# Splitting a mixture-of-experts pass at the tenth weight half: a first pass under a scan, a pass over all tokens, and a rest

## The reference

```python
u  = x @ Wi.T + bi;  sp = x @ Ws.T + bs             # 128 states
def step(state, inp):                               # one after the other, 2048 times
    u_t, sp_t = inp
    state = jnp.tanh(state @ A.T + u_t @ B.T) + sp_t
    return (state, state @ C.T)
x = layernorm(x + ys @ Wo.T + bo)
# experts: D = 1024, H = 4096, E = 8, the two best by softmax of x @ gate_w.T
h = relu(einsum('nd,edh->neh', x, w1) + b1)
y = einsum('neh,eho->neo', h, w2) + b2
x = layernorm(x + einsum('ne,neo->no', dense_gate, y))
# layer 1: causal attention with 16 heads, then a gated feed-forward
```

## Time and profile before

| | us |
|---|---|
| two runs | 8627.08 and 8993.85, median 8810.46 |
| profiled execution | 8637.14 |
| its span, slowest core (1) | 8635.5 |
| spans of its cores | 8619.6 to 8635.5 |

### The profile page before, as it was taken

How to read it: one execution, slowest core, us unless ns; L and a number is a source line. 1 busy time by engine, 2 the same in 40 slices (tenths; PEclk the granted TensorE clock), 3 DMA queues, 4 the chain that set the end, 5 groups by cost and what they waited for, 6 DMA issues and landing times.

```text
span 8635.5 us, 83834 instructions; the slowest of 8 cores (8619.6 to 8635.5 us)
## 1 busy us (share of the span) xinstructions
PE 5770.1 (67%) x24427; PEld 2317.4 (27%) x24427; DVE 2788.6 (32%) x4299; ACT 1541.8 (18%) x3342; POOL 431.5 (5%) x676
## 2 busy tenths in 40 slices
PE   2256666676648989888889899834556455645545
PEld 1122222222223434333333344311112111211111
DVE  0021111111232222222222222244554555445555
ACT  2312222222200010100100101012112211221111
POOL 0001111111000000000000000000000000000000
PEclk6579899899859999999999999965556555555677
DMA  1035555555313222233232222210000000000012
GB/s 45 0 52 77 77 78 77 78 77 78 65 27 49 41 40 40 40 48 50 48 49 41 40 40 40 40 11 5 10 10 6 5 10 10 6 5 5 0 19 50
DMA packets 181047, 321.74 MB, mean 37 GB/s; under 512 B 67222, under 2 KB 67734, under 8 KB 178582
## 3 DMA queue, kind: packets, MB, share of 16 engines
q0 software_dynamic: 170240, 284.34, 21.9%
q1 hardware_dynamic: 10390, 32.04, 1.2%
HBM read 583.71 MB, written 8.39 MB: 69 GB/s over the span
## 4 chain that ended last, share of the span: by engine, by line
PE 43%; DMA 27%; DVE 15%; issue 8%; ACT 5%; DVEq 1%; ACTq 0%; POOLq 0%; SPq 0%; PEldq 0%
PE psA L1024 37%; DMA w1b<-w 12%; DMA w2c<-w 8%; DMA w1f<-w 6%; PE psB L1024 6%; DVE mcols L1024 4%; ACT tanh_bf L1024 2%; ACT PT L1024 2%; DVE xA L1024 2%; DVE Qpair L1024 1%; DVE qraw L1024 1%; DVE mtmp L1024 1%; DVE rowT L1024 1%; DVE mcol L1024 1%; ACT rowT L1024 1%
## 5 line engine op out<-in xcount | busy, mean ns | idle before, releaser
L1024 PE MATMUL psA<-xS,w1b 128*128 128x512 bf16 x7168 | 1716.6, 388 | 353.8 <-DMA w1b<-w 344.2
L1024 PE MATMUL psA<-hbuf,w2c 128*128 128x512 bf16 x8192 | 1785.1, 380 | 70.5 <-DVE hbuf L1024 70.5
L1024 DVE TENSOR_SCALAR hbuf<-psA,b1c 128x512 bf16<-128x512 f32 x512 | 384.5, 751 | 2590.1 <-PE psA L1024 2590.1
L1024 PEld LDWEIGHTS psA<-hbuf,w2c 128*128 128x128 bf16 x8192 | 791.7, 98 | 1040.2 <-issue 100.2
L1024 PEld LDWEIGHTS psA<-xS,w1b 128*128 128x128 bf16 x7168 | 682.7, 99 | 1123.3 <-issue 418.2
L1024 ACT ACTIVATE tanh_bf<-psB,c_n 128x1 bf16<-128x1 f32 x2047 | 538.8, 263 | 1428.6 <-PE psB L1024 1428.6
L1024 PE MATMUL psB<-tanh_bf,AT_s 128*128 128x1 bf16 x2047 | 336.4, 164 | 493.3 <-ACT tanh_bf L1024 452.7
L1024 ACT ACTIVATE hbuf<-psA,b1c 128x512 bf16<-128x512 f32 x512 | 351.8, 687 | 1279.7 <-PE psA L1024 1264.2
L1024 PE MATMUL psA<-xS,w1f 128*128 128x512 bf16 x1024 | 340.5, 392 | 257.4 <-DMA w1f<-w 248.0
L1024 ACT ACTIVATE PT<-psA 128x512 bf16<-128x512 f32 (+3 forms) x448 | 308.6, 689 | 1023.2 <-PE psA L1024 1011.4
L1024 PEld LDWEIGHTS psB<-tanh_bf,AT_s 128*128 128x128 bf16 x2047 | 201.5, 98 | 1049.8 <-issue 1037.8
(11 more groups left out here) (155 smaller groups left out, 3787.5 us busy)
## 6 DMA issues: line engine op xcount, KB each, us to landing
w2c<-w POOLq DMA_DIRECT2D x256, 512.0 KB, 5.3
w1b<-w POOLq DMA_DIRECT2D x192, 512.0 KB, 5.3
w1f<-w POOLq DMA_DIRECT2D x128, 256.0 KB, 4.2
xA<-xT SPq DMA_DIRECT2D x8, 1024.0 KB, 16.7
out<-ost SPq DMA_DIRECT2D x8, 1024.0 KB, 12.7
xA<-xT SPq DMA_DIRECT2D x8, 768.0 KB, 13.2
Qh<-Qpair SPq DMA_DIRECT2D x16, 256.0 KB, 3.4
Kh<-Qpair SPq DMA_DIRECT2D x16, 256.0 KB, 3.4
```

Source lines behind the costliest of these rows:

```text
L1024: ins = getattr(eng_obj, method)(*args, **kw)
```

## The change

The first pass over tile 0 stops after KA = 10 of the 16 halves. Then scan output, norm and gate of tiles 1 to 3 are done as before, and the rest comes in two calls: the last six halves for all four tiles, and the first ten halves for tiles 1 to 3. `moe` takes the tiles, the list of halves and `pp` as arguments. The 1536 scan steps are spread over 10 x 152 = 1520 hooks instead of 16 x 152 = 2432. A call that finds earlier matmuls makes its first w1 load wait for them. Every token still meets every half once; six of the 32 loads of a half are gone (26 are left).

```diff
     CH_NTS = ((0,), (1, 2, 3))
+    KA = 10
...
-    def moe(ch, hook=None):
-        nts = CH_NTS[ch]
-        pp = (ch == 0)
+    def moe(nts, halves, pp, hook=None):
         w1done = {}
         zw = (("zin", V("zin")),)
-        w1_load(HALVES[0][0], HALVES[0][1], w=zw)
+        if V("mm1") > 0:
+            zw = zw + (("mm1", V("mm1")),)
+        w1_load(halves[0][0], halves[0][1], w=zw)
         w1done[0] = V("w1l")
         mm2_slice = None
-        for hi, (e, half) in enumerate(HALVES):
+        for hi, (e, half) in enumerate(halves):
...
-            if pp and hi + 1 < len(HALVES):
-                e2, h2 = HALVES[hi + 1]
+            if pp and hi + 1 < len(halves):
+                e2, h2 = halves[hi + 1]
...
-            if not pp and hi + 1 < len(HALVES):
-                e2, h2 = HALVES[hi + 1]
+            if not pp and hi + 1 < len(halves):
+                e2, h2 = halves[hi + 1]
                 w1_load(e2, h2, w=(("mm1", V("mm1")),))
...
-            mark(f"moe_c{ch}")
-            nhooks = 16 * len(CH_NTS[0]) * (16 * 9 + 8)
-            per = [0]
-
-            def hook(per=per, ch=ch):
-                if ch == 0:
+            if ch == 0:
+                mark("moe_c0")
+                nhooks = KA * (16 * 9 + 8)
+                per = [0]
+
+                def hook(per=per):
                     per[0] += 1
                     tgt = TS + ((T - TS) * per[0]) // nhooks
                     scan_pump(tgt - scan_cursor[0])
-            moe(ch, hook=hook)
-            if ch == 0:
+                moe(CH_NTS[0], HALVES[:KA], pp=True, hook=hook)
                 scan_pump(T - scan_cursor[0])
+            else:
+                mark("moe_mix")
+                moe((0, 1, 2, 3), HALVES[KA:], pp=False)
+                mark("moe_c1")
+                moe(CH_NTS[1], HALVES[:KA], pp=False)
             barrier()
```

## The result

| | before | after |
|---|---|---|
| median of all runs, us | 8792.71 (29 runs) | 8740.86 (30 runs) |
| lowest, us | 8624.07 | 8545.44 |
| profiled execution, us | 8637.14 | 8575.5 |
| spans of its cores, us | 8619.6 to 8635.5 | 8535.9 to 8574.1 |

The ratio after to before is **0.9927, with a 95% interval of 0.9895 to 0.9959**: a small gain, 0.7%, well inside the 2% named in the prediction. Forecast was 8557 / 8637 = 0.9907, which lies in the interval. But 8741, the median, lies above the range given, 8490 to 8660. The two medians hold executions in which the cores of one die, or of both, were granted a lower clock, and which take up to 9137.97 and 9126.2 us; the ratio leaves them out. The two lowest times differ by 78.6 us.

A forecast was written before the change was run, and what follows sets the result against it. The load queue was taken to bound the first phase, the scan's chain after the change. Saving 422.0 us there and adding 341.9 in mixed halves gives -80.1 on the profiled 8637.14: 8557 us, range 8490 to 8660.

The forecast's parts named there:

- What bounds the kernel, and what comes next: First phase: bound passes from loads, 109.7 us a half, to the scan's chain, 130.9 us a half on PE.
- Loads hidden: First phase: loads cost nothing; tightest is w1f of half 1, with 6 us to spare.
- Clock: First phase: clock may fall in w1 stages, costing 2.4 us per half at the w2 stage start, 24 in all.
- a thinner stage costs nothing in itself: First-phase w1 stages: at the lower clock a step with one large matmul behind it still takes 0.67 us.
- Mixed halves: Six halves with four tiles: one more tile each at 56.98 us, 341.9 us added, nothing new exposed.
- Seams: Starts of the mixed phase and of the last ten halves: taken as nothing, bounded by 8 us.
- dense stretch: Rival, chance 0.05: mixed halves' longer dense PE work, 230 us against 173, is throttled; 342 us more, 8899 us.
- The rest of the kernel taken as untouched: Stages between the phases and all after them: unchanged, 0 us.
- The time itself and its range: Whole kernel: 8557 us for an execution like the profiled one, range 8490 to 8660, 0.5% for the spread of runs.
- the late loads: Rival, chance 0.05: in the first phase w1f arrives late on five halves, 155 us more, 8712 us.
- the low clock: Rival, chance 0.06: clock stays low through ten first-phase w2 stages, up to 27.8 us each, 278 in all, 8811 us.
- the first rival: Rival, chance 0.04: loads still set the first phase's pace, which would save 658 us there, 8321 us.

The follow-up runs named there:

- scan-first run: The changed kernel with all remaining 1536 scan steps made before the ten halves instead of between their matmuls; spans of 9158.8 to 9170.6 us.
- spread run: The changed kernel with a scan hook also after each of the 128 w2 matmuls; 8338.23 us at best, timed again 8365.16 us median, ratio 0.9656.
- thirteen halves: The changed kernel with thirteen first-phase halves instead of ten, three mixed, gate row fetched at the first half of every call; ratio 0.9873 to the kernel before.
- warm: The changed kernel with one unused 128x512 matmul into an idle PSUM bank after each w1 matmul of the first phase; ratio 0.9859 to the kernel before.
- eight-half split: The changed kernel with eight halves in the first phase instead of ten and eight in the mixed one; ratio 0.9959 to the kernel before.
- ka13warm: The split at thirteen halves with one unused 128x512 matmul after every fourth w1 matmul of the first phase; ratio 0.9903 to the kernel before.

## Why the prediction was right in its parts and wrong in its time

| term, us (core 5 against core 1 before) | predicted | measured |
|---|---|---|
| a half of the first phase | 130.9 + 2.4 = 133.3 | 132.2 (mean of nine) |
| first phase | 1330.3 | 1320 |
| saved there | 422.0 | 432 |
| w2 stage with its clock loss | 30.3 | 29.3 to 30.8 |
| a mixed half | 248.7 | 248.5 |
| a half of the last ten | 191.7 | 191.0 |
| end of all halves, against before | -80.1 | -97.6 |
| everything after them | 0 | +36 (core 5), -4 (core 1) |

The column compares two different cores. Each core against itself, the halves end 67 to 100 us earlier, 86 on the mean of the eight, and 85 on core 5. So the sum of -80.1 us was nearer than the column shows: the parts are right.

*What bounds the kernel, and what comes next.* Right. The bound of the first phase passed from the loads to the scan's chain, and the long DMA waits fell from nine to the opening one. The scan-first run and the spread run show the two limits apart, 109 and 132 us a half.

*Loads hidden.* Right, the tightest case too: w1f of half 1 was there when PE came at 680.88 (0.2 us of wait are put down to it). At thirteen halves, where PE comes earlier, it was not, and cost 14 us.

*Clock.* Right in direction and nearly in size: it fell to 0.50 in the w1 stages, and `warm` prices it at 21 us in the w2 stages against the 24 taken. On cores 6 and 7, where it came back to 0.81 only, it cost 15 to 17 us more. But the remark that a thinner stage costs nothing in itself held only because ten halves give 1.01 steps per hook. At thirteen, where some steps have two matmuls behind them, the same low clock took most of what I expected. What a low clock costs thus depends on the split.

*Mixed halves.* Right to 0.2 us. Seams and the dense stretch too: in the mixed halves the granted clock stood at 1.00 (core 5, 2400 to 2600 us):

```profile
2400.00:2600.00 200.00, 195.42 (x901) 87.47 (x900) 59.15 (x83) 21.03 (x31) 5.12 (x8) 1.00 0.13 21
```

*The rest of the kernel taken as untouched.* Wrong by 36 us on the slowest core. Nothing there was edited, and core 1 shows no loss. The difference is in the last feed-forward, its first two and its third matrix, in windows of core 5 and then of core 1:

```profile
8175.00:8361.00 186.00, 136.61 (x512) 55.45 (x512) 61.75 (x105) 39.49 (x65) 13.98 (x16) 0.73 0.22 22
8361.00:8430.00 69.00, 68.62 (x256) 27.68 (x256) 43.10 (x63) 0.00 (x0) 5.24 (x6) 0.80 0.28 28
8366.00:8433.00 67.00, 65.03 (x246) 26.02 (x244) 43.23 (x63) 0.85 (x1) 5.24 (x6) 0.81 0.24 24
```

```profile
8170.00:8338.00 168.00, 118.18 (x512) 48.82 (x512) 61.49 (x104) 39.53 (x65) 13.44 (x16) 0.84 0.24 24
8339.00:8398.00 59.00, 57.08 (x254) 22.72 (x253) 42.31 (x62) 0.00 (x0) 5.24 (x6) 1.00 0.33 32
```

Same instructions, clock 0.80 against 1.00: 255 us against 228, which is 27 of the 40 us by which core 5's rest exceeds core 1's. The low figure is not a mean of two levels: the third window, cut from the stage, stands at 0.81 throughout. Core 4 shows the same there; cores 6 and 7, of the same die, stand at 0.97 and 1.00 in that window. Why two cores were granted less in this execution no run settles. It is not tied to the edit, since the other cores of the same execution and all eight cores of the eight-half split, whose profiled spans differ by under 10 us, don't show it, and since other kernels do: it is on cores 6 and 7 of the second spread execution, in the same last stages. It is why the slowest core gained 61 us and the cores of die 0 82 to 99.

*The time itself and its range: the step that failed.* The prediction put its sum on the profiled execution (8637.14), said that the median shown, 8810.46, was pulled up by its other run, and gave 0.5% to the spread of runs. With 29 runs the median before is 8792.71: the figure taken as pulled up was the typical one. Of the 30 executions after, which span 8545.44 to 9126.2 us, 18 lie above the upper bound of 8660, and so does their median of 8740.86; of the 29 before, 19 lie above 8660. The two runs at hand already differed by 4.3%. So the term that was mis-sized is the spread, 0.5% where the runs span 6.8%, and with it the choice of what to forecast; the edit's own share, -80.1 us, was right against the two lowest times (-78.6). Had it been taken from the median shown, 8730 would have come out, 11 us from the measured median. That would have been luck: the two medians differ by 51.85 us only, and the shown one lay 18 above that of the 29 runs. Also, the upper bound of 8660 does not take in "a third" of the rivals, as the prediction says, but two thirds of the late loads (103 of 155 us over 8557) and nearly half of the low clock (127 of 278 over 8533); and the saving by the first rival is 1752.3 - 1097 = 655 us, not 658.

What makes the executions differ can be seen in `warm`, whose profiled execution took 8890.75 us. I had named a throttled dense stretch as a rival at 0.05, as a consequence of the change. A throttle is there, but it comes and goes between executions of one program, and something like it before the change as well: executions of that kernel of over 9100 us show a mean granted clock of 0.71 on the cores of one die against 0.79 on the other. One stretch of the mixed halves, of core 0 and of core 3, both of die 0:

```profile
2200.00:2300.00 100.00, 97.71 (x371) 39.94 (x370) 26.27 (x36) 6.79 (x10) 2.12 (x3) 0.81 0.11 17
2200.00:2300.00 100.00, 97.71 (x451) 43.62 (x449) 31.97 (x45) 9.44 (x14) 0.00 (x0) 1.00 0.00 1
```

At 0.81 PE makes 371 matmuls in the time of 451, with next to no wait in either. The first phase of core 0 took 1355 us in this execution instead of 1304, and its halves ended 350 us later than those of cores 4 to 7. That the long executions without a trace come from the same level is not shown, but their low mean clocks fit it. The Trainium skill ("TensorE: Matmul & The Clock Gate", Part 1) states that a current limit takes the whole die to 13/16 of the clock, 0.8125, once three of its cores run dense matmuls. The level agrees with these rows, so "No row of this profile agrees", in the prediction, held for that one profile only. The condition does not agree: before the change all eight cores stood at 1.00 in the window of the earlier trace rows, and here cores 0 and 1 stood at 0.81 while cores 2 and 3 of the same die stood at 1.00 in the same work. What sets it off no run shows.

## What to carry to other kernels

When work is laid between the steps of a serial chain, count how many steps fall in each stage: a stage that carries few of them (8 in 28 us here) is paid in full, and spreading the steps evenly was worth 207 us, more than twice the change itself. It was worth 20 while another queue held the phase, so find the pace of each queue alone before choosing. And where two runs of the same program differ by 4%, a sum made on one trace predicts the difference between like executions, not the median of the runs.

## What the runs showed of the hardware that I had not expected

More TensorE work made a phase shorter. With thirteen halves, 32 unused matmuls of 128x512 per half raised the granted clock of the first w1 stage from 0.61 to 0.92, most w2 stages fell from as much as 30.9 to 27.9 us, and the phase from 1496 (core 1) to 1453 us (core 7). The price of two large matmuls between two scan steps is nothing at 2.4 GHz and 0.17 us at 1.2 GHz (0.84 against 0.67). A fitting reason, from the same traces, is that such a matmul takes 0.42 us at the low clock, so that two of them outlast the step of 0.67: steps with three behind them took 1.26 us at the low clock and still 0.67 at the full one (`ka13warm`, core 5).

The second surprise was a third level of the granted clock, 0.81, beside the two of the kernel before, 0.50 and 1.00. In the ten profiled executions it shows in five, of five different kernels, and there always on two neighbouring cores together (0 and 1, 2 and 3, 4 and 5, 6 and 7), for 100 us in all on cores 6 and 7 after the change and for some 3000 us on cores 0 and 1 of `warm`. A core at 0.81 is neither idle nor waiting; its work is the same and slower by the clock, 371 matmuls for 451.
